# Two causal self attentions: the added mask replaced by extra contraction rows and 32x32 corner products, and their later steps issued one step sooner

## What is computed

```python
scores = jnp.einsum('bhqd,bhkd->bhqk', q, k) / math.sqrt(Dh)
causal = jnp.tril(jnp.ones((S, S), dtype=bool))
scores = jnp.where(causal, scores, -jnp.inf)
attn = jax.nn.softmax(scores, axis=-1)
out = jnp.einsum('bhqk,bhkd->bhqd', attn, v)
```

## Time and profile before

| | |
|---|---|
| median of 3 runs | 581.05 us (575.83 to 585.4) |
| the profiled execution | 578.1 us, span of the core 576.3 us |
| PE | 538.5 us busy, 93% of the span, 4933 products |
| DVE | 364.7 us, 63% |
| POOL | 316.7 us, 55% |
| ACT | 259.5 us, 45% |
| granted TensorE clock, mean | 0.994 |
| `SELF0` in the profile | first mask product at 36.70 us, last mask products at 76.38 us |
| `SELF1` in the profile | first mask product at 325.55 us |
| first `CROSS` mask product | 385.93 us |

### The profile page before, as it was taken

The page is one execution under the profiler, slowest core; times in us unless marked ns, Lnnn a source line. Parts: engine busy times, 40 slices in busy tenths (PEclk is TensorE's granted clock), DMA queues, the critical chain, the costliest instruction groups (busy, mean ns, idle before and its releaser), DMA issues. The chain is left out here.

```text
span 576.3 us, 13097 instructions
## 1 busy us (share of the span) xinstructions
PE 538.5 (93%) x4933; PEld 343.2 (60%) x4933; DVE 364.7 (63%) x798; ACT 259.5 (45%) x533; POOL 316.7 (55%) x392
## 2 busy tenths in 40 slices
PE   6999998999999999999988989987999998989998
PEld 4556765445656666665665556654555554456687
DVE  5456864999864746452486578757687766963331
ACT  2325453000395666653445345645566567204530
POOL 3438754989675454330033579859899983450000
PEclk9999999999999999999999979999999999999999
DMA  7996029000008333332304992011130013018311
GB/s 221 165 129 278 3 80 388 1 0 1 0 7 217 114 106 97 105 97 61 101 15 62 126 250 86 3 28 30 35 97 1 3 29 138 1 65 306 132 41 63
DMA packets 25134, 53.05 MB, mean 92 GB/s; under 512 B 3515, under 2 KB 16333, under 8 KB 23153
## 3 DMA queue, kind: packets, MB, share of 16 engines
q1 hardware_dynamic: 24357, 51.01, 32.3%
q10 hardware_dynamic: 716, 1.21, 0.7%
HBM read 41.51 MB, written 1.12 MB: 74 GB/s over the span
## 5 line engine op out<-in xcount | busy, mean ns | idle before, releaser
L1396 PE MATMUL PS<-R 128*128 128x256 f16 (+5 forms) x1864 | 185.4, 275 | 2.7 <-DVE R L1298 1.4
L1396 PEld LDWEIGHTS PS<-R 128*128 128x128 f16 (+4 forms) x1864 | 123.8, 103 | 71.6 <-issue 43.2
L1141 DVE TENSOR_REDUCE mx<-PS 128x4 bf16<-128x512 f32 x128 | 82.3, 684 | 36.5 <-PE PS L1396 26.7
L831 ACT ACTIVATE R<-PS 128x512 f32<-128x512 f32 x128 | 69.3, 593 | 69.6 <-PE PS L1396 69.5
L614 POOL TENSOR_TENSOR R<-mx,causal 128x512 bf16<-128x512 bf16 x64 | 66.8, 1065 | 37.4 <-DVE mx L1141 36.3
L1396 PE MATMUL PS<-xnT,R 128*128 128x512 f16 (+1 forms) x348 | 83.3, 379 | 1.4 <-ACT xnT L745 1.4
L614 POOL TENSOR_TENSOR R<-mx,R 128x512 bf16<-128x512 bf16 x64 | 65.3, 1042 | 7.3 <-DVE mx L1141 7.2
L1289 DVE TENSOR_TENSOR R<-R,wr 128x512 f32<-128x512 f32 (+1 forms) x46 | 33.8, 734 | 56.1 <-ACT R L930 52.6
L930 ACT ACTIVATE R<-PS,small 128x512 f32<-128x512 f32 (+1 forms) x50 | 34.2, 685 | 48.0 <-PE PS L1396 47.9
L1396 PEld LDWEIGHTS PS<-xnT,R 128*128 128x128 f16 (+1 forms) x348 | 33.8, 99 | 33.5 <-ACT xnT L745 2.0
L1396 PE MATMUL PS<-negidb,R 128*128 128x128 bf16 x512 | 42.7, 222 | 3.6 <-ACT R L831 1.8
(11 more groups left out here) (206 smaller groups left out, 820.0 us busy)
## 6 DMA issues: line engine op xcount, KB each, us to landing
R<-in_experts_dram SPq DMA_DIRECT2D x5, 1536.0 KB, 7.5
R<-R SPq DMA_DIRECT2D x48, 128.0 KB, 6.7
wr<-g_scr SPq DMA_DIRECT2D x16, 256.0 KB, 3.2
R<-in_w_dram SPq DMA_DIRECT2D x1, 3200.0 KB, 17.4
R<-in_w_dram SPq DMA_DIRECT2D x1, 3168.0 KB, 10.1
WT<-in_wt_a_dram SPq DMA_DIRECT2D x2, 1024.0 KB, 12.3
R<-in_toe_dram SPq DMA_DIRECT2D x1, 2048.0 KB, 12.7
wr<-g_scr SPq DMA_DIRECT2D x10, 192.0 KB, 2.7
```

Of the source, the lines that this page charges most:

```text
L831: s.activation(PTm[:, n % 4, 4 * k:4 * k + 4, :], bank(2 + (2 * n + k) % 3).rearrange("p (h q) -> p h q", h=4), ACT.Exp, scale=c["sc"]).th ...
L1141: v.tensor_reduce(mx[:, n % 4, 4 * k:4 * k + 4], bank(k).rearrange("p (h k) -> p h k", h=4), AX.X, ALU.max).then_inc(S("att_mx"), 1)
L1396: return nc.tensor.matmul(o_, l, r, start=start, stop=stop)
```

## The change

- The self attentions no longer add a mask product. The queries and keys get 4 more contraction rows (48 becomes 52), held at partitions 48 to 51 and 112 to 115. Four query rows hold +65504 in blocks of 32 queries and four key rows hold -65504 for all keys of later blocks, so the score product itself gives a very large negative number for every key block after the query's block.
- What is left to mask are the four 32x32 blocks on the diagonal. `on_diagonal` adds them with 4 products of 32x32 identity and corner, 128 columns each (4 heads of 32), one for each quarter of the partitions. That is 8 products for the by-query banks (`later_keys`) and 8 for the by-key bank pair (`later_keys_by_key`) for each unit. The by-key score gets its own mask, since it no longer comes in through `LMs`.
- POOL no longer forms `LMs` for the self attentions. `less_max` reads the maximum itself, a column broadcast to 128 columns, as the stationary operand, and waits for DVE and not for POOL. `CROSS` is unchanged in this.
- `unit_at` gives the self attentions every stage from lag 2 on one step sooner. In the step the order for a self unit is: `less_max`, `scores_by_key`, then `scores` and `later_keys` of the new unit, then `later_keys_by_key`. `CROSS_FROM` is 19, `QUERIES` moves by one step.
- POOL builds the 4-row constants at the start, two transfers of the SP queue park them in DRAM (repeated), and four bring them to the rows of `SELF0`, all ahead of the ctxT load; four more do so for `SELF1` behind the last product of the first expert layer (`down0`), ahead of `stack(SELF1)`. `pe` waits for them before a self attention's first unit.
- Four filler products in front of the first `less_max` of a run are gone.

```diff
-CROSS_FROM = 20
+CROSS_FROM = 19
...
-                u = t - start - lag
+                u = t - start - (lag if c is CROSS or lag < 2 else lag - 1)
...
-            return [(8 * (u % 2) + 2 * j + k, 64 * k, 48, 4 * (u % 2) + j) for k in range(2) for j in range(4)]
+            return [(8 * (u % 2) + 2 * j + k, 64 * k, 52, 4 * (u % 2) + j) for k in range(2) for j in range(4)]
...
+            def later_blocks(c):
+
+                for which, to in ((0, QS), (1, c["KS"])):
+                    for row in (48, 112):
+                        sp.dma_start(to[row:row + 4, :, :].rearrange("p g t -> p (g t)"),
+                                     blocks_scr[which]).then_inc(S("blocked"), 16)
+
+            sp.wait_ge(S("blocks"), 1)
+            for which in range(2):
+                sp.dma_start(blocks_scr[which].rearrange("p (a t) -> p a t", t=P),
+                             blocks[:, which:which + 1, :].broadcast_to([4, 8 * B, P])).then_inc(S("blocks_parked"), 16)
+            sp.wait_ge(S("blocks_parked"), 32)
+            later_blocks(SELF0)
             sp.wait_ge(S("w_a0"), 16)
             load(ctxT[:, :, :], A["ctxT"], "ctxT_loaded")
...
+            sp.wait_ge(S("down0"), N0)
+            later_blocks(SELF1)
             stack(SELF1)
...
-                        if n >= 4:
-                            dve.wait_ge(S("att_lm"), 2 * (n - 3))
+                        if c is CROSS and u >= 4:
+                            dve.wait_ge(S("att_lm"), 2 * (u - 3))
+                        elif n >= 4:
+                            dve.wait_ge(S("att_st"), n - 3)
...
+                def on_diagonal(i, row, corner):
+
+                    rows = slice(row, row + QUARTER)
+                    for first in range(0, P, QUARTER):
+                        cols = slice(first, first + QUARTER)
+                        ins = mm(PS[cols, i, :].rearrange("p (j w) -> p j w", j=4)[:, :, cols], identb[rows, rows],
+                                 corner[rows, rows].unsqueeze(1).broadcast_to([QUARTER, 4, QUARTER]), False, True)
+                    return ins
+
+                def later_keys(c, u):
+                    for k in range(2):
+                        ins = on_diagonal(k, QUARTER * k, causal)
+                    ins.then_inc(S("att_s"), 1)
+
+                def later_keys_by_key(c, u):
+                    n = number(c, u)
+                    for k in range(2):
+                        ins = on_diagonal(2 + (2 * n + k) % 3, QUARTER * (2 + k), causal_k)
+                    ins.then_inc(S("att_st"), 1)
...
-                        if (c, u) == (run[0][0], 0) and k == 1:
-                            keep_busy(4, 2 + (i + 1) % 3)
-                        pe.wait_ge(S("att_lm"), i + 1)
+                        if c is CROSS:
+                            pe.wait_ge(S("att_lm"), 2 * u + k + 1)
+                        else:
+                            pe.wait_ge(S("att_mx"), i + 1)
                         if i >= 3:
                             pe.wait_ge(S("att_exp"), i - 2)
                         for j in range(4):
-                            mm(PS[:, 2 + i % 3, j * P:(j + 1) * P],
-                               LMs[:, n % 3, 4 * k + j, :], negidb[:, :], j == 0, False)
+                            most = (LMs[:, n % 3, 4 * k + j, :] if c is CROSS
+                                    else mx[:, n % 4, 4 * k + j:4 * k + j + 1].broadcast_to([P, P]))
+                            mm(PS[:, 2 + i % 3, j * P:(j + 1) * P], most, negidb[:, :], j == 0, False)
...
                     c, u = unit_at(run, t, 0)
+                    if older and older is not CROSS:
+                        scores_by_key(older, of)
                     if c:
-                        mask(c, u)
+                        operands_ready(c, u)
+                        if c is CROSS:
+                            mask(c, u)
                         scores(c, u)
-                    if older:
+                    if c and c is not CROSS:
+                        later_keys(c, u)
+                    if older is CROSS:
                         scores_by_key(older, of)
+                    elif older:
+                        later_keys_by_key(older, of)
```

More of the change, by code:

```diff
@@ L33 @@
 FAR = -3.0e38
+HUGE = 65504.0
+QUARTER = 32
 HF = 512
@@ L603, in attention @@
                     c, u = unit_at(run, t, 0)
[L604 to L608, removed]
+                    if c is CROSS:
+                        pool.wait_ge(S("xmask"), 2)
                         n = number(c, u)
-                        if n >= 3:
-                            pool.wait_ge(S("att_st"), n - 2)
+                        pool.wait_ge(S("att_st"), n - 2)
                         for k in range(2):
@@ L1489, in attention, with operands_ready @@
             def attention(run):
-                def mask(c, u):
-                    upb = c["upb"]
-                    b, first = divmod(u, upb)
+                def operands_ready(c, u):
+                    b, first = divmod(u, c["upb"])
                     if c is CROSS and first == 0 and b % 2 == 0:
@@ L1503, in mask @@
                         pe.wait_ge(S("qx_lo"), 2)
-                    m_ = mask_of(c, b)
+                    if c is not CROSS and u == 0:
+                        pe.wait_ge(S("blocked"), 64 * (1 + ATTENTIONS.index(c)))
+                def mask(c, u):
                     n = number(c, u)
                     for k in range(2):
-                        if n >= 1:
-                            pe.wait_ge(S("att_mx"), 2 * n + k - 1)
-                        mm(bank(k), identb[:, :], m_.unsqueeze(1).broadcast_to([P, 4, P]), True, False)
+                        pe.wait_ge(S("att_mx"), 2 * n + k - 1)
+                        mm(bank(k), identb[:, :], xmask[:, u // c["upb"], :].unsqueeze(1).broadcast_to([P, 4, P]), True, False)
+                def on_diagonal(i, row, corner):
[14 more added lines that the diff above has]
+                    ins.then_inc(S("att_st"), 1)
                 def scores(c, u):
+                    n = number(c, u)
                     ts = slice(u // c["upb"] * P, (u // c["upb"] + 1) * P)
@@ L1515, in scores @@
                         for k in range(2):
+                            if c is not CROSS and j == 0 and n >= 1:
+                                pe.wait_ge(S("att_mx"), 2 * n + k - 1)
                             _, row, rows, idx = unit_heads(c, u)[4 * k + j]
                             ins = mm(PS[:, k, j * P:(j + 1) * P], QS[row:row + rows, idx, ts],
-                                     c["KS"][row:row + rows, key_at(c, idx), ts], False, j == 3)
-                    ins.then_inc(S("att_s"), 1)
+                                     c["KS"][row:row + rows, key_at(c, idx), ts], c is not CROSS and j == 0,
+                                     c is CROSS and j == 3)
+                    if c is CROSS:
+                        ins.then_inc(S("att_s"), 1)
                 def less_max(c, u):
@@ L1548, in scores_by_key @@
                             _, row, rows, idx = unit_heads(c, u)[4 * k + j]
-                            ins = mm(PS[:, 2 + (2 * n + k) % 3, j * P:(j + 1) * P], c["KS"][row:row + rows, idx, ts],
-                                     QS[row:row + rows, idx, ts], False, j == 3)
-                    ins.then_inc(S("att_st"), 1)
+                            mm(PS[:, 2 + (2 * n + k) % 3, j * P:(j + 1) * P], c["KS"][row:row + rows, idx, ts],
+                               QS[row:row + rows, idx, ts], False, False)
                 def pv(c, u):
@@ L1653, in attention @@
                     elif not any(unit_at(run, t, lag)[0] for lag in range(4)):
-                        keep_busy(13 if run is FIRST and t == 24 else 3, 4)
+                        keep_busy(13 if run is FIRST and t == 23 else 3, 4)
                     if t == 0:
```

26 lines of the change are left out of this document (20 added, 6 removed).

## The result

| | before | changed |
|---|---|---|
| median of 19 runs each | 578.47 us (574.58 to 587.68) | 582.29 us (577.81 to 587.83) |
| ratio | | 1.0062, 95% interval 1.0034 to 1.009 |
| span of the profiled execution | 576.3 us | 577.3 us |
| mean granted clock in it | 0.994 | 0.982 |
| first product of `SELF0` | 36.70 us | 41.97 us |

The change costs 0.6%, 3.8 us between the medians, well inside the 2% that the prediction took as the least to be told from no change. The time is within the range and near the predicted 581.5, but not for the predicted reasons.

A forecast was written before the change was run, and what follows sets the result against it. PE was taken as the bound in the steady self attentions. Terms 2.2 + 1.2 + 1.2 - 1.0 - 0.8 - 0.8 = +2.0 gave 580.1 from the profile, 583.05 from the median; middle 581.5 us, range 571 to 593.

The forecast's parts named there:

- Setup transfers: Before SELF0 and SELF1: parking and fetching constants ahead of the stacks is covered by several us; cost 0.
- Late by up to 3: Start of SELF0: should the first stack be late beyond its cover, SELF0 would start late by up to 3 us.
- Corner products: Self units where PE is full: 16 products take 0.44 plus 0.10 for a change of form; +0.11 a unit, +2.2 us.
- In a full step PE has 1.5 to 2 us behind the corner products: Full self-attention steps: this PE work covers the 1.29 + 0.16 us, so the ring is just hidden there.
- the ring: First self-attention steps: PE and DVE wait on each other through less_max, scores, corner products and maxima; 2.73 us a step.
- The rival of corner products one after another: Self units: the corner products run serially, +0.44 over the price in some 26 units, +11.4 to 593 us; chance 9%.
- less_max with a broadcast column: Self units: the repeated-column stationary operand loads like the tile before, 0.44 us, so nothing is added.
- First steps: SELF0's start: step 6 begins at about 15.6 us, plus 0.8 for the missing unit, against 15.2 before; +1.2 us.
- POOL's waits: Turns of a batch in SELF1: PE's 0.62 us wait for LMs and a later smaller one go; -1.0 us.
- Tail of SELF0: End of SELF0: PE's idle 0.80 us may go, as the exponential is a step further ahead; -0.8 us.
- Gap before CROSS: Before CROSS: transfers land 0.8 us earlier in PE's work, so 0.8 of the 1.60 wait stays; -0.8 us.
- SELF1's first steps: SELF1's start: 15.6 + 1.0 for DVE's constants + 3.0 for a clock fall + 0.8, against 19.2 before; +1.2 us.

The follow-up runs named there:

- e7: The kernel before with only the change's setup added (constants, parking and fetch transfers, ctxT behind them, PE's wait); 583.24 us, ratio 1.0105 to before.
- e12: e11 without the 16 corner products of a unit, so the diagonal blocks are not masked; 566.98 us against 575.74.
- e11: e6 with SELF0's constant rows written by POOL, ACT and DVE instead of transfers, parking for SELF1 behind ctxT; 575.74 us, ratio 0.997 to before.
- e9: e6 with the later stages at their old lags and CROSS starting at step 20 again; 579.83 us, ratio 1.0069 to before.
- e6: e5 with 7 filler products after the corner products in steps 1 and 2 of each self attention; 576.97 us, ratio 0.9998 to before.
- e13: e11 with DVE's second-half copies moved behind the values and 6 fillers behind the second and fourth turn; 574.61 us, ratio 0.9954 to before.
- e10: The kernel before with 4 filler products in steps 3 and 4 of each run of attentions; 577.56 us, ratio 1.0013 to before.
- e5: The changed kernel with parking after the first weights landed, fetches between the halves of SELF0's stack, ctxT behind both; 579.43 us, ratio 1.0052 to before.

## Why the prediction was right in its number and wrong in its steps

- **Setup transfers, costed at 0: the step that failed.** They cost 5.3 us of start in the profile, and e7 gives 1.05%. The error is "stacked halves have several us before step 0": no row showed how much cover the landing had, only that PE did not wait. I counted when the transfers are issued, which moved by 1.3 us, and not how long they take to land, which went from 6.1 to 10.3. Nor did I add what a wait of 5.9 does to the clock. "Late by up to 3" was the right mechanism with too small a bound.
- **Corner products, the term mis-sized.** Predicted 0.44 and one more change of form, 0.10; measured 0.21 together. The change of form is in it, and right. Within the 0.21 the records of the 16 products start over 0.05, 3 to 4 ns apart, and pv starts 0.155 behind the last, of which a product of 128 columns is 0.055. That leaves 0.10 for the change and 0.05 + 0.055 = 0.11 for the products, where I had 0.44; the lower bound, 0.06, was near. A unit is 0.22 cheaper, not 0.11 dearer: for 20 units -4.4 in place of +2.2. I had taken the price from scores and pv, of which only two or four places of the array work side by side; the 16 corner products hold 16 different 32x32 places, which I did not count. e12 confirms the 0.21.
- **"In a full step PE has 1.5 to 2 us behind the corner products"**: wrong for a step with only pv and four turns, which the earlier trace rows already have at 1.07. There the ring shows and the gain is lost. From step 6 on SELF0 gains 1.1 and not 2.2 (104.38 - 58.55 = 45.8 to the convolution, before 98.03 - 51.88 = 46.2 with 0.8 less to score), and SELF1 loses 1.4 of its gains in three steps (from 348.29, 351.06 and 357.40), of which 0.6 is a stall inside pv at 353 whose cause is not seen: +2.5 that the sum does not have.
- **The rival of corner products one after another** is refuted: 0.21 is far below its limit of 0.85. The row-group rule of the Trainium skill (TensorE: Matmul & The Clock Gate, Part 3) would have made it likely; this trace disagrees with it: the 16 products load weights of their own, four in a row to each row group, and these loads too start 3 to 4 ns apart while the first product runs.
- **less_max with a broadcast column**: right, 0.44 and 0.10 for the change of form behind it.
- **First steps**: the ring is as described, 2.61 where 2.73 was summed, but the sum took the wrong place in it. Step 6 begins with the first half of less_max, which follows the first bank's maximum, and that comes 1.5 behind SELF0's first product and not 2.13. With the clock at 1.00 throughout, in e11, step 6 begins at 14.5 (54.34 - 39.82) and not 15.6: +0.1 in place of +1.2. In the changed kernel, where the wait has taken the clock down, it begins at 16.6 (58.55 - 41.97): +2.2. SELF1's begins 16.53 us after its first product (348.29 - 331.76) where the sum had 19.6. The clock fell as expected (0.55 from 338 to 345), but cost 1.4 and not 3.0: at 1.00 throughout e11 takes 15.16 (343.22 - 328.06) for the same steps. With 0.8 for the missing unit the changed kernel has 17.3 against 19.2 before: -1.9, not +1.2.
- **POOL's waits**: right, both are gone.
- **Tail of SELF0**: wrong. The 0.79 is there in every profile, also without corner products. Its releaser was "issue", so the row named nothing that a sooner exponential could end; what holds PE there stays open.
- **Gap before CROSS**: right in direction. All of 1.60 is gone, not half, but this is not firm: e11 has 1.12 again, e12 0.65.

The measured terms are 5.3 (start), 2.2 (SELF0's first steps), -4.4 (corner products), 2.5 (full steps in which the ring or a stall shows), -1.9 (SELF1's first steps), -1.0 (POOL) and -1.6 (gap): +1.1, where the profiled executions differ by +1.0. So large errors of opposite sign, the setup above all and the corner products, met near the predicted number. That it came out near was luck. Not in the sum is the clock of a usual run, by which the 1.0 us between the profiled executions becomes 3.8 between the medians. Mean time of the runs with the same mean granted clock (number of runs; those that a ratio leaves out are left out here too, and the kernel before is taken from the runs beside the experiments):

```
clock           before       changed     e9          e6          e13
0.970 to 0.974               583.7 (5)
0.979                        581.9 (8)               583.3 (1)
0.982           581.5 (1)    578.7 (2)   583.2 (2)
0.985                        577.8 (1)   580.8 (4)
0.988           581.3 (2)                579.4 (5)               579.5 (1)
0.991           579.4 (18)               578.4 (1)   578.3 (2)   577.4 (1)
0.993, 0.994    577.3 (27)                           576.9 (6)   576.7 (3)
0.997           575.8 (11)                           575.4 (2)   574.3 (4)
1.000           574.0 (10)                                       573.1 (3)
```

The kernel before loses 1.5 to 2.1 us for 0.003 of mean clock between its well filled rows. At 0.982 the changed kernel is 2.8 us faster, in spite of its late start, but that is two runs against one. What is firm is where the runs lie: 13 of these 16 of the changed kernel have 0.979 or less, 66 of 69 of the kernel before 0.991 or more. At 0.991 e9 and e6 take the same, one run against two. A fall in the ring can cost less than one where PE is full (1.4 us for SELF1's above, of 3.0 expected), so the same clock does not mean the same loss. All this fits a change that does less work and is then granted a slower engine, since it makes PE wait at its start and in its first steps; it does not prove it.

## What to carry to other kernels

Cost a transfer by when its last byte lands, with what else is in flight, and not by when it is issued; small constants that an idle engine can write should not go through the queue that feeds the next stage. Where a change gives TensorE idle time, look at the granted clock of the steps behind it, and price the fillers that keep it up: they were worth about 0.5% in the new order and nothing in the old. A profile is one execution, so don't read an edit's effect on the clock from one of them. Products that take different 32x32 places of the array cost far less than their number suggests, but count them also in a ring that waits for another engine, where they stand on the path. And add up what a step has to hide a wait, for the shortest step and not for the usual one.

## What the runs showed of the hardware

- 16 products of 32x32 with 128 columns each, in 16 different places of the array, start over 0.05 us and take 0.21 from the first one's start to the next group's; e11 and e12 differ by 0.21 a step. The starts are 3 to 4 ns apart. The Trainium skill (TensorE: Matmul & The Clock Gate, Part 3, on packing small matmuls) has about 4 ns between products in different places, and the trace agrees.
- ACT writes 4096 half-precision columns in 3.62 us and DVE copies as many in 1.19 to 1.50.
- A start with 1.4 us of idle time before the second turns was followed by a clock of 0.59 in one kernel (e10, 16 products in 8.8 us), and one with 1.62 in another by 1.00 (the changed kernel, 7.1). e5 (1.35 idle, then 0.50, 10.2 us) and e6 (1.24, then 1.00, 7.1) do the same work up to there. So neither the length of one wait nor the kernel decides.
